# Attention and quantised FFN layer on one core: the row maxima turned by VectorE instead of TensorE, the division by the softmax sums on VectorE instead of GpSimd

## What is computed

```python
x = x + xattn(layernorm(x), ctx, Wq, bq, Wk, bk, Wv, bv, Wo, bo)   # 8 heads of 16, rope on half of each head
x = x + ffn(layernorm(x), w_gate, w_up, w_down)
# xattn: softmax(q k^T / 4) v per head over 512 x 512 scores, then Wo
# ffn:   gate, up = bitlinear(x, w_gate), bitlinear(x, w_up)       # 512 -> 2048
#        out = bitlinear(fwht(silu(gate) * up), w_down)            # 2048 -> 512
# bitlinear(x, w) = act_quant(x) @ weight_quant(w).T   (per-token absmax, 8 bits; ternary weights)
```

## Time and profile before

| | |
|---|---|
| time, 3 runs | 1508.82 us median (1507.08 to 1510.89) |
| profiled execution | 1509.78 us, its span 1508.0 us |
| busy PE / DVE / ACT / POOL | 94% / 82% / 77% / 71% of the span |
| granted TensorE clock | 0.975 of full speed on average |

### The profile page before, as it was taken

The page is one execution under the profiler, slowest core; times in us unless marked ns, Lnnn a source line. Parts: engine busy times, 40 slices in busy tenths (PEclk is TensorE's granted clock), DMA queues, the critical chain, the costliest instruction groups (busy, mean ns, idle before and its releaser), DMA issues.

```text
span 1508.0 us, 31029 instructions
## 1 busy us (share of the span) xinstructions
PE 1414.5 (94%) x11042; PEld 743.4 (49%) x11042; DVE 1229.5 (82%) x2149; ACT 1168.6 (77%) x2033; POOL 1069.9 (71%) x803
## 2 busy tenths in 40 slices
PE   2678999999999999999999999999999999999985
PEld 1214455455555544555555445555555455555443
DVE  2757788888888888888888888988888888888744
ACT  4586778888788888887788788877887888877663
POOL 3122788777777788777777887777778877777662
PEclk9677999999999999999999999999999999999998
DMA  8852344333344443323434433323344433333000
GB/s 211 225 116 46 58 72 77 62 65 62 61 74 68 78 78 64 66 62 60 77 64 78 78 64 71 60 64 69 64 78 78 72 64 63 64 52 64 16 8 15
DMA packets 81113, 108.13 MB, mean 72 GB/s; under 512 B 9664, under 2 KB 59200, under 8 KB 79936
## 3 DMA queue, kind: packets, MB, share of 16 engines
q1 hardware_dynamic: 77744, 93.56, 34.6%
q10 hardware_dynamic: 3216, 12.58, 2.4%
HBM read 38.73 MB, written 8.39 MB: 31 GB/s over the span
## 4 chain that ended last, share of the span: by engine, by line
PE 79%; ACT 9%; DVE 4%; DMA 3%; issue 3%; SPq 1%; POOL 1%; POOLq 0%; ACTq 0%; DVEq 0%
PE pv L495 15%; PE ring L536 14%; PE s L480 13%; PE s L454 13%; PE ring L574 7%; PE ring L550 6%; PE ring L428 4%; ACT region L726 4%; PE ring L504 2%; PE ring L442 2%; DMA region<-parts 2%; PE ring L561 1%; ACT parts L821 1%; ACT xqT L735 1%; ACT y_last L769 1%
## 5 line engine op out<-in xcount | busy, mean ns | idle before, releaser
L1035 DVE TENSOR_REDUCE maxima<-s 128x1 bf16<-128x512 f32 x1024 | 671.1, 683 | 110.4 <-PE s L454 107.8
L726 ACT ACTIVATE region<-s 128x512 f32<-128x512 f32 x1024 | 570.4, 594 | 101.0 <-PE s L480 93.0
L454 PE MATMUL s<-region 96*128 96x512 bf16 x1024 | 369.3, 390 | 26.2 <-DVE maxima L1035 13.5
L1293 POOL TENSOR_TENSOR region<-region,th 128x512 f32<-128x512 f32 x126 | 158.9, 1273 | 293.8 <-DVE th L1130 292.1
L480 PE MATMUL s<-region 97*128 97x512 bf16 x1024 | 357.8, 384 | 7.6 <-ACT region L726 4.0
L495 PE MATMUL pv<-region,v_ext 128*17 128x512 f32 x2048 | 264.2, 599 | 0.0
L292 POOL TENSOR_TENSOR region<-region 128x512 f32<-128x512 f32 x189 | 240.6, 1273 | 12.5
L293 POOL TENSOR_TENSOR region<-region 128x512 f32<-128x512 f32 x189 | 241.1, 1275 | 0.0
L454 PEld LDWEIGHTS s<-region 96*128 96x128 bf16 x1024 | 95.0, 98 | 207.3 <-DVE maxima L1035 110.9
L480 PEld LDWEIGHTS s<-region 97*128 97x128 bf16 x1024 | 91.0, 98 | 172.7 <-ACT region L726 140.0
L290 POOL TENSOR_TENSOR region<-region 128x1024 f32<-128x1024 f32 x63 | 148.0, 2371 | 3.4 <-DVE region L293 3.4
(11 more groups left out here) (111 smaller groups left out, 1862.5 us busy)
## 6 DMA issues: line engine op xcount, KB each, us to landing
region<-parts SPq DMA_DIRECT2D x384, 128.0 KB, 4.3
x_in<-in_x SPq DMA_DIRECT2D x32, 256.0 KB, 2.7
c_in<-in_ctx SPq DMA_DIRECT2D x32, 256.0 KB, 3.0
rope_c<-region SPq DMA_DIRECT2D x64, 128.0 KB, 2.3
x_res<-in_x SPq DMA_DIRECT2D x32, 256.0 KB, 2.9
out<-o_sb SPq DMA_DIRECT2D x32, 256.0 KB, 4.7
region<-in_wg_t ACTq DMA_DIRECT2D x1, 2048.0 KB, 8.9
region<-in_wu_t ACTq DMA_DIRECT2D x1, 2048.0 KB, 7.6
```

The costliest lines, as they stand in the source:

```text
L454: pe.matmul(s1[p][:, :], q_stack[k][0:STACK, h, 128 * c:128 * (c + 1)], k_stack[k][0:STACK, h, :], start=True, stop=True).then_inc(s1_full ...
L726: act.activation(probs[:, n % 8, :], s2[n % 2][:, :], ACT.Exp, scale=SCALE).then_inc(exp_done, 1)
L1035: dve.reduce_max(maxima[:, c, h:h + 1], s1[p][:, :], AXX).then_inc(s1_max[p], 1)
L1293: pool.tensor_tensor(zj, zj, th[:, j % 2, :], ALU.mult).then_inc(glu_done, 1)
```

## The change

VectorE now makes `maxima` in fp32, in the order head by chunk, turns it by one instruction in 32x32 blocks (`turned_max`), and negates it into bf16 (`neg_max`, now 128x32); both belong to the new `turn_max`. `stack_max` writes row 96 in four DMAs of 2 KB, one for each 32 partitions, in pieces of 64 bytes. `max_transpose`, `max_out` and the ring entry `mT` are gone. `mix` is gone from GpSimd, its multiplication is the last instruction of `normalise`.

```diff
-RING = {"yT0": 4, "yT1": 4, "down": 4, "wo": 2, "v": 0, "y0": 3, "mT": 1, "y1": 3, ...
+RING = {"xqT": 2, "gate0": 2, "up0": 2, ... "yT0": 3, "yT1": 3, "down": 3, "wo": 1, "y0": 2, "v": -1, "y1": 2, "y2": 2, "y3": 2, "hg": 1}
...
-        maxima = sb("maxima", [128, KC, NH], BF16)
-        neg_max = sb("neg_max", [NH, T], BF16)
+        maxima = sb("maxima", [128, NH, KC], F32)
+        turned_max = sb("turned_max", [128, NH * KC], F32)
+        neg_max = sb("neg_max", [128, NH * KC], BF16)
...
             def stack_max(b):
-                moved(sp, "mT", b)
+                sp.wait_ge(max_ready, b + 1)
                 sp.nop(nofuse=True)
-                sp.dma_start(q_stack[slot(b)][STACK:STACK + 1, :, :], neg_max[:, :]).then_inc(max_stacked, 16)
+                row = q_stack[slot(b)][STACK:STACK + 1, :, :].rearrange("p h (c i q) -> p i (h c) q", c=KC, i=4)
+                for i in range(4):
+                    sp.dma_start(row[:, i], neg_max[32 * i:32 * (i + 1), :]).then_inc(max_stacked, 16)
...
+            def turn_max(b):
+                for p in range(2):
+                    dve.wait_ge(s1_max[p], 16 * (b + 1))
+                dve.transpose(turned_max[:, :], maxima[:, :, :].rearrange("p h c -> p (h c)")).then_inc(max_turned, 1)
+                dve.wait_ge(max_turned, b + 1)
+                wait(dve, max_stacked, 64 * b)
+                dve.tensor_scalar(neg_max[:, :], turned_max[:, :], -1.0, None, ALU.mult).then_inc(max_ready, 1)
...
             def normalise(b, g):
                 dve.reciprocal(inv_sum[:, :], blocks[:, :, DH]).then_inc(inv_done, 1)
+                dve.wait_ge(inv_done, 2 * b + g + 1)
+                if g == 0:
+                    wait(dve, attn_done, b)
+                dve.tensor_tensor(mixed[:, :].rearrange("p (n g e) -> p n g e", g=2, e=DH)[:, :, g, :],
+                                  blocks[:, :, 0:DH], inv_sum[:, :].unsqueeze(2).to_broadcast([128, 16, DH]),
+                                  ALU.mult).then_inc(mixed_done, 1)
```

More of the change, by code:

```diff
@@ L475, in scores @@
                 if n == 0:
[L476 removed]
+                    pe.wait_ge(max_stacked, 64 * (b + 1))
                 if n == 0 and b == 0:
@@ L621, in step @@
[L621 to L632 removed]
                 xq_transpose(t - 2)
[L634 removed]
+                scores(t - 1, 2)
@@ L653, in step @@
                 project(t + 1, "k")
-                gate_up(t - 2, "gate", 2)
                 scores(t - 1, 9)
+                score_max(t, 8)
                 scores(t - 1, 10)
-                score_max(t, 8)
+                weigh(t - 1, 1)
                 score_max(t, 9)
-                weigh(t - 1, 1)
                 scores(t - 1, 11)
                 score_max(t, 10)
+                gate_up(t - 2, "gate", 2)
                 scores(t - 1, 12)
+                scores(t - 1, 13)
                 score_max(t, 11)
@@ L674, in step @@
                 scores(t - 1, 17)
                 gate_up(t - 2, "up", 3)
-                gate_sum(t + 1)
-                score_max(t, 15)
+                score_max(t, 17)
                 scores(t - 1, 18)
+                scores(t - 1, 19)
+                score_max(t, 18)
+                weigh(t - 1, 3)
+                scores(t - 1, 20)
+                scores(t - 1, 21)
+                y_transpose(t - 3, 0)
+                score_max(t, 19)
+                score_max(t, 20)
+                scores(t - 1, 22)
@@ new lines, in step @@
+                scores(t - 1, 23)
+                weigh(t - 1, 4)
+                scores(t - 1, 24)
+                score_max(t, 21)
+                scores(t - 1, 25)
+                score_max(t, 22)
+                weigh(t - 1, 5)
+                scores(t - 1, 26)
+                score_max(t, 23)
+                scores(t - 1, 27)
+                score_max(t, 24)
+                scores(t - 1, 28)
+                score_max(t, 25)
+                scores(t - 1, 29)
+                y_transpose(t - 3, 1)
@@ new lines, in step @@
+                scores(t - 1, 30)
+                score_max(t, 26)
+                score_max(t, 27)
+                scores(t - 1, 31)
+                weigh(t - 1, 6)
+                score_max(t, 28)
+                weigh(t - 1, 7)
+                score_max(t, 29)
+                up_sum(t)
+                score_max(t, 30)
+                down(t - 3, 0, 4)
+                down(t - 3, 4, 8)
+                down(t - 3, 8, 12)
+                score_max(t, 31)
+                down(t - 3, 12, 16)
@@ L680, in _ @@
+                attn_out(t - 1)
+                hadamard(t - 2, 0)
+                project_v(t + 1)
+                score_max(t + 1, 0)
+                hadamard(t - 2, 1)
+                hadamard(t - 2, 2)
+                score_max(t + 1, 1)
+                hadamard(t - 2, 3)
+                score_max(t + 1, 2)
+                scores(t, 0)
+                bias_product(t + 1)
+                scores(t, 1)
+                score_max(t + 1, 3)
+                gate_rows(t - 1)
             for t in range(FIRST, LAST):
@@ L955, in step @@
                 exps(t, 0)
                 exps(t, 1)
-                sign_piece(t - 1, 2, 3)
+                abs_piece(t, 2, 0)
+                xqT_out(t - 1)
+                exps(t, 2)
+                gate_rows_out(t - 1)
+                exps(t, 3)
+                norm1_apply(t + 2)
+                exps(t, 4)
+                exps(t, 5)
+                tanh(t - 1, 0)
+                abs_piece(t + 2, 0, 0)
+                sign_piece(t + 1, 0, 0)
+                sign_piece(t - 2, 2, 7)
@@ L959, in _ @@
+                round_y(t - 2, 1)
+                sign_piece(t, 1, 3)
+                exps(t, 10)
+                abs_piece(t + 1, 1, 0)
+                sign_piece(t - 1, 2, 6)
             for t in range(FIRST, LAST):
```

303 lines of the change are left out of this document (101 added, 202 removed).

## The result

The changed kernel takes 1638.25 us (median of 4 runs, 1636.33 to 1639.0), the kernel before 1509.86 us in the same comparison (4 runs, 1507.08 to 1512.69). The ratio is 1.0848, 95% interval 1.0825 to 1.0872. The forecast was 1568 within 1512 to 1588: the sign was right, the loss, 128 us, is more than twice the 59 that were forecast, and it lies outside the range and above every rival of the forecast (the highest was 1596). The profiled execution took 1639.0 us, its span 1637.1; the granted clock was 0.949 of full speed on average, before it was 0.975.

A forecast was written before the change was run, and what follows sets the result against it. TensorE's instruction list was taken as the bound, 42.88 us per batch. Less 0.2 for list work, plus 0.8 for multiplication 0 and 1.5 for the negation: 45.0, 59 us more over 28 periods, 1568 us, range 1512 to 1588.

The forecast's parts named there:

- every rival of the forecast: Lock doesn't bite, 1501 us, 0.17; only multiplication 0 pays, 1526, 0.12; only negation pays, 1545, 0.13; transfers late, 1596, 0.08.
- product 0: First VectorE multiplication of a batch, behind `weigh` 3; forecast to make TensorE wait 0.8 us.
- W: Time mark: the end of `weigh` 7 in a batch, from which later starts are counted.
- product 1: Second VectorE multiplication of a batch, behind `weigh` 7; forecast to cost nothing.
- The list work: Reordered engine lists and dropped transposes: 0.2 us less per period, between 0.7 less and 0.3 more.
- The marks: Predicted TensorE times in a batch: `attn_out` at W + 4.2, `scores` 0 at W + 10.3, gate at W + 12.65 without the negation's wait.
- G: Time mark: the gate start of a batch; forecast 30.1 us before W, without added waits.
- multiplication 0: VectorE's product behind `weigh` 3: waits 1.5 us for GpSimd's `rest`, works 0.42, makes TensorE wait 0.8 us.
- Multiplication 1: VectorE's product behind `weigh` 7: waits for `third_part`, ends at W + 2.1, covered by `down` and maxima, no cost.
- The negation: VectorE's fp32 to bf16 negation of the maxima: waits 1.5 us for `hadamard_last`, delays `residual`, costs 1.5 us per period.
- The four DMAs: Transfers behind the negation: last lands at W + 11.2 to 11.7, delaying `scores` 0 beside `residual`'s wait, adding nothing.
- The rule: VectorE and GpSimd share ports under an exclusive lock; the other is blocked for a whole instruction; applied to products and negation.

The follow-up runs named there:

- the product one maximum later: Changed kernel with VectorE's first product of a batch moved behind the maximum of block 19, no pause on GpSimd: 1584.56 us, ratio 1.0494.
- The pause one instruction further on: Changed kernel with an added GpSimd semaphore wait between the first L292 and L293 of the second `hadamard_half`: 1585.67 us, ratio 1.0501.
- with the pause: Changed kernel with one added GpSimd wait on a semaphore for its own `rest`, before the second `hadamard_half`: 1549.34 us, ratio 1.0256.
- with the turn: Changed kernel with a 32x32 block turn of 128x256 on VectorE in place of the product, division left out: 1536.43 us, ratio 1.0169.
- The scaling with one input: Changed kernel with VectorE multiplying by a constant in place of the product, division by the sums left out: 1627.38 us, ratio 1.0783.

## Why the forecast was right in its sign and wrong in its size

**Where the 128 us are.** Along one line of kernels, by their medians, which come from several comparisons (the kernel before had 1509.86 to 1511.53 in them, so each step is good to some 2 us): the new way of the maxima without the negation costs 3 us (old lists); with the new lists and the product on GpSimd it is 16, so the lists cost some 12; the negation adds 48 (1525.67 to 1573.78); the product on VectorE adds 64.5 (to 1638.25). In the kernel after itself the parts stand otherwise, as waits hide one another. Per period, 4.7 us in 22 of 25 batches: 2.7 TensorE's wait behind product 0, 1.4 the lower clock behind that wait (8.8 us for 7.44 from the wait's end to W), 0.5 product 1 (13.0 for 12.52 from W to the gate), and 0.1 that is left. The three batches at the full clock and with a short product 1 show that rest by itself: 45.72 is 0.14 more than 42.88 and 2.70. The negation costs nothing there.

**The list work** was forecast at 0.2 us less and is 0.3 to 0.4 more, with the product on GpSimd. The transposes' 0.3 us did not come back: in the old lists without them the period is 42.97. Part of the loss is the wait for the last Hadamard stage, 0.4 us in that kernel. This I had not looked at. In the kernel after, GpSimd isn't waited for there, and the lists with all that is not listed above cost 0.14 us together; the 0.2 less of the forecast shows in no kernel.

**The marks** held: `attn_out` at W + 4.12, `scores` 0 at W + 10.17, the gate at W + 12.52, W being 831.90 (forecast 4.2, 10.3, 12.65 without the negation's wait). This is the batch with a short product 1; in the 22 others the median is W + 4.3 for `attn_out` and W + 13.0 for the gate. One sum was off by its own terms: G to W, said to be 30.1, comes to 29.9 (31.1 less 0.87, less two `scores` of 0.23, and 0.1 more for `weigh`), and is 30.5 without the stand-still (798.69 to 831.90, less 2.70).

**The step that failed is multiplication 0.** The text said that GpSimd's `rest` "holds until G + 22.4. VectorE waits 1.5 us and works 0.42", and so "TensorE waits 0.8 us". The moment of asking was right, 0.67 us into `rest`; the end of the wait was not. VectorE was passed over twice and waited 3.8 us, TensorE 2.70 for 0.8. I had read from the earlier trace rows that VectorE is served when GpSimd's instruction is through. It was so there, even with the next GpSimd instruction ready, but a few such meetings couldn't show that it is always so, and in the kernel after it isn't. The two added pauses show that this is the cause: with one behind `rest` the product takes 1.72 us, close to the 1.9 that the forecast's rule gives, and with one behind L292 2.97.

**The clock** is a part that the sum had no term for. A stand-still of 2.70 us was followed by the lower level in 22 of 25 batches, of 1.48 us in 6 of 25, of 1.50 us in the product one maximum later in none of 26. It makes 1.4 us of the 4.7.

**Multiplication 1** was forecast at no cost ("had the wait been above 1.3 us, each further tenth would be paid"), and this is the second step that failed. It waits 0.9 to 1.1 us in most batches and costs about 0.5, some 0.2 ahead of `attn_out` and 0.3 behind it. The forecast had followed `attn` alone, which was ready in time; but the maxima and `residual` stand behind the product in the same list, and their cover is used up earlier. The pause one instruction further on parts this from the clock: there, at the full clock and with a product 1 of 1.8 us, `attn_out` is at W + 4.73 and the gate 8.67 behind it, and at the lower clock and with one of 0.45 us at W + 4.12 and 8.40 behind it. The cover by `down` is real in part: in the old lists, without it, TensorE stood 0.91 us.

**The negation** was forecast to wait 1.5 us and cost 1.5. In the kernel after it waits for nothing, because the wait of product 0 holds TensorE and VectorE and not GpSimd: `hadamard_last` ends at 835.77, 1.4 us before the negation is asked for, and 3.5 before it in most batches. Take product 0's wait away and it returns: 1.7 us with the product on GpSimd, 1.0 with the pause, 1.2 with the turn. The mechanism and its size were right, its place in the sum wasn't, since the two terms are not independent: a longer first wait moves the marks for the second. The forecast had shifted W by its own 0.8 us only.

**The four DMAs** are hidden, as forecast. They leave SyncE in 3.12 us (0.78 apart; 0.61 to 0.73 had been taken), land after 1.7, and made TensorE wait once in 12 batches for 0.4 us. The 2.0 us that the forecast took from the Trainium skill, "DMA: Bandwidth & Descriptors", stand there in the section on the anatomy of a DMA issued by GpSimd, and that page has short pieces slow for HBM only; these go from SBUF to SBUF and are issued by SyncE, so the 1.7 of the trace is what counts.

```profile
837.77 3.12 SPq L352 DMA_DIRECT2D region<-neg_max  x4
...
region<-neg_max SPq DMA_DIRECT2D x128, 2.0 KB, 1.7
...
PE s L470 <- DMA region<-neg_max: 0.4, 1, 0.4
```

**The rule.** The Trainium skill, "SBUF — State Buffer", on the two separate sides, says that the side that starts first has the ports for its whole instruction. The trace agrees: no product or negation here ran beside a GpSimd instruction, 0.14 us of overlap aside. The scaling with one input waited like the product with two, and the turn in blocks didn't wait. The loss came from what I added to it, that the waiting engine is next.

## What to carry to other kernels

Before moving an instruction to VectorE, look at what GpSimd does at that moment and for how long it runs without a semaphore wait: price the wait to the end of that run, not of one instruction, unless a trace shows the turn being taken. Where such a wait can't be avoided, a wait on a semaphore on GpSimd is cheap and lets VectorE in, but each one shifts the next meeting. Price waits in their order, since the first one moves all that follow; and count the clock with a long stand-still of TensorE: here 2.7 us cost 1.4 more. And follow a late result through everything that stands behind it in its engine's list, not only to its own reader.

## What the runs showed of the hardware

- A VectorE product or negation waiting for GpSimd was passed over at 287 of 336 changes between GpSimd instructions other than into the 128x1024 of `hadamard_last`, was let in at all 202 of those, and at all 437 gaps above 0.04 us. Most of these are a few meetings, each repeated batch after batch. What decides at a change is open: asked for 0.26 us into L292 it was let in at the change to L293, 0.41 us into it it wasn't, and in the last batches of the kernel after, 0.30 and 0.73 us into it, it was.
- An fp32 to bf16 `tensor_scalar` of 128x32 waited up to 1.7 us for GpSimd; turns in 32x32 blocks of 128x256 (0.45 us), 128x512 (0.70) and 128x32 (0.20) beside a busy GpSimd did not.
- Behind a stand-still of 2.70 us TensorE's granted clock was 0.66 over the next 5 us in 22 of 25 batches and 1.00 again in the 5 us after; behind 1.48 us it fell in 6 of 25, behind 1.50 us in another kernel in none of 26.
